# State-space blocks of 8 channels x 16 states, and experts with two input banks and one output bank, in a two-layer sandwich kernel

## The reference

```python
u, z = split(x @ W_in.T)
uc = silu(conv3(u) + conv_b)
proj = uc @ W_xproj.T            # B: 16 columns, C: 16 columns, dt: 8 columns
delta = softplus(dt @ W_dt.T + b_dt)
A = -exp(A_log)                  # 256 x 16
def step(h, inp):                # over the 1024 positions
    h = exp(d_t[:, :, None] * A) * h + (d_t * u_t)[:, :, None] * b_t[:, None, :]
    return h, einsum('bdn,bn->bd', h, c_t)
y = (ys + uc * D) * silu(z)
return y @ W_out.T
```

## Time and profile before

| | |
|---|---|
| runs, median of 3 (lowest, highest) | 3173.7 us (3173.47, 3174.76) |
| profiled execution, its own time | 3170.2 us |
| its span, first to last instruction | 3168.4 us |
| mean granted TensorE clock | 0.866 of full |
| PE busy | 2407.0 us (76%) |
| DVE busy | 2311.8 us (73%) |
| ACT busy | 1678.5 us (53%) |
| POOL busy | 1263.5 us (40%) |
| chain that ended last | PE 46%, DVE 20%, issue 18%, POOL 11%, ACT 4% |

### The profile page before, as it was taken

How to read it: one execution, slowest core, us unless ns; L and a number is a source line. 1 busy time by engine, 2 the same in 40 slices (tenths; PEclk the granted TensorE clock), 3 DMA queues, 4 the chain that set the end, 5 groups by cost and what they waited for, 6 DMA issues and landing times.

```text
span 3168.4 us, 41094 instructions
## 1 busy us (share of the span) xinstructions
PE 2407.0 (76%) x14962; PEld 1690.2 (53%) x14962; DVE 2311.8 (73%) x4141; ACT 1678.5 (53%) x2552; POOL 1263.5 (40%) x1203
## 2 busy tenths in 40 slices
PE   3114776667676696899999999999999388667867
PEld 1002444344344564577777777776777366245635
DVE  3994798699599612688878878887888533874386
ACT  4223663665376242678777877787778124022402
POOL 0341143144124200365766576667667540114011
PEclk8556878888788898799999999999999789788978
DMA  3000000000000000100000100010000100000000
GB/s 99 0 0 0 0 1 1 1 1 1 1 1 1 1 1 14 41 21 21 24 21 21 28 21 21 24 29 21 21 21 1 40 1 1 0 14 1 1 0 14
DMA packets 32026, 41.96 MB, mean 13 GB/s; under 512 B 8897, under 2 KB 18130, under 8 KB 31442
## 3 DMA queue, kind: packets, MB, share of 16 engines
q1 hardware_dynamic: 31826, 39.34, 4.6%
HBM read 12.05 MB, written 2.10 MB: 4 GB/s over the span
## 4 chain that ended last, share of the span: by engine, by line
PE 46%; DVE 20%; issue 18%; POOL 11%; ACT 4%; SPq 1%; DMA 1%; POOLq 0%; DVEq 0%; ACTq 0%
PE ps L954 10%; PE ps L932 6%; PE ps L943 6%; POOL MA L379 5%; PE ps L710 3%; DVE MA L1090 3%; DVE MA L1410 3%; PE ps L914 2%; DVE lnb L265 2%; PE ps L1724 2%; PE ps L645 2%; PE ps L1711 2%; PE ps L647 1%; PE ps L646 1%; PE ps L1648 1%
## 5 line engine op out<-in xcount | busy, mean ns | idle before, releaser
L1090 DVE TENSOR_REDUCE MA<-ps 128x1 f32<-128x1024 f32 x512 | 623.1, 1220 | 190.4 <-PE ps L932 177.6
L379 POOL TENSOR_TENSOR MA<-MA,BIG 128x1024 f32<-128x1024 f32 x120 | 280.1, 2355 | 624.3 <-DVE BIG L350 624.3
L954 PE MATMUL ps<-MA,WB 128*64 128x128 f32 x4096 | 504.5, 277 | 0.0
L954 PEld LDWEIGHTS ps<-MA,WB 128*64 128x64 f32 x4096 | 442.8, 137 | 88.4 <-issue 87.4
L344 DVE TENSOR_TENSOR_SCAN BIG<-BIG 128x1024 f32<-128x1024 f32 x128 | 346.8, 2748 | 0.0
L932 PE MATMUL ps<-BIG 96*128 96x512 f16 x1024 | 312.6, 387 | 13.3 <-DMA BIG<-WB 4.9
L632 ACT ACTIVATE HR<-ps,b 128x512 f32<-128x512 f32 x288 | 191.5, 686 | 244.0 <-PE ps L647 243.0
L710 PEld LDWEIGHTS ps<-WB,HR 128*128 128x128 f32 x2304 | 305.8, 209 | 25.0 <-issue 8.7
L710 PE MATMUL ps<-WB,HR 128*128 128x128 f32 x2304 | 312.8, 294 | 0.0
L1017 ACT ACTIVATE WB<-ps,MA 128x1024 f32<-128x1024 f32 x206 | 229.5, 1114 | 149.3 <-DVE MA L1090 147.5
L497 PE MATMUL ps<-bc,sel 96*128 96x512 bf16 x256 | 108.2, 520 | 249.1 <-DVE BIG L350 190.7
(11 more groups left out here) (286 smaller groups left out, 5133.2 us busy)
## 6 DMA issues: line engine op xcount, KB each, us to landing
BIG<-BIG SPq DMA_DIRECT2D x192, 64.0 KB, 2.0
BIG<-WB SPq DMA_DIRECT2D x192, 64.0 KB, 2.0
WB<-w_dram SPq DMA_DIRECT2D x1, 2304.0 KB, 14.6
X<-x_dram SPq DMA_DIRECT2D x4, 512.0 KB, 12.5
HR<-w_dram SPq DMA_DIRECT2D x1, 2048.0 KB, 9.3
out_dram<-X SPq DMA_DIRECT2D x4, 512.0 KB, 3.2
WB<-wqkv_dram SPq DMA_DIRECT2D x1, 1536.0 KB, 6.1
WB<-w_dram SPq DMA_DIRECT2D x2, 512.0 KB, 8.2
```

The source lines that it names most:

```text
L379: e.tensor_tensor(yy[:, c, :], yy[:, c, :], db[n % 2][c], ALU.add).then_inc(*p_my.up(b, n, c))
L954: x = e.matmul(bank[6][64 * pp:64 * pp + 64, 0:128], V[(4 * b + g) % 2][:, k, 64 * pp:64 * pp + 64], DT[n % 2][:, 128 * k:128 * k + 128], ...
L1090: e.tensor_reduce(L_of(n)[:, c:c + 1], ps[s][:, :], AX, ALU.max, negate=True).then_inc(*v_amx.up(n, s))
```

## The change

**Blocks instead of states.** The 256 x 16 pairs of a channel and a state are cut in 32 blocks `j` of 128 partitions, 8 channels with 16 states each. B and C no longer change from block to block: their 128-partition copies `Brep` and `Crep` are made once a batch by matmuls with repeated columns of `wx` (`bc`). What changes is delta and delta times u: both are split in three bf16 parts by ACT and POOL (`part`, `rest`), stored to DRAM, read back stacked as 96 partitions (`sin`), and broadcast to the 16 partitions of each channel by a matmul with `esel` (`dl` to bank 2, `du` to banks 0 and 1). ACT's exponential reads bank 2, half by half, and writes a ring of seven tiles. DVE multiplies by B in place in PSUM (`tb`), the scan reads its second operand from PSUM, POOL multiplies by C (`th`), and PE sums over the states with the f32 matrix `ysel` into banks 4 and 5 (`y`, for two blocks at a time). z and the convolved u are kept in DRAM between use and come back before the D term.

**One list of events.** `mamba_events` writes the planned times of all engines. The next batch's preparation is planned inside the loop of the batch before (30 us after its start), and the splitting of the expert weights inside the first loop. All small state-space matmuls share bank 2, each waiting for the reader before (`m_freed`). A loop is planned at 4.4 us a block in the first batch and 6.1 in the others; experts of batch b are planned from 36 us after its last block.

**Expert banks.** Inputs use banks 3 and 6 in turn, outputs bank 7 alone, so that the products of an expert wait for the sum of the one before.

The core of the diff:

```diff
-M_PERIOD, N_PERIOD = 181, 6.8
+S_AT, TT = [58.0], [4.4, 6.1, 6.1, 6.1]
+for _t in TT:
+    S_AT.append(S_AT[-1] + 32 * _t + 4)
+PRE_AT = [(0.0, 1.0), (S_AT[0] + 30, 2.0), (S_AT[1] + 30, 3.0), (S_AT[2] + 30, 3.0)]
-    return M_AT["rnorm"] + 1 + F_PERIOD * b + F_AT[what] + more
+    return S_AT[b] + 31 * TT[b] + 36 + F_AT[what] + more
...
+                for j in range(32):
+                    t = T0 + P * j
+                    for h in range(2):
+                        g = T0 + P * (j - j % 4) - 8.8 + 1.1 * (2 * (j % 4) + h)
+                        if b == 0 and j < 4:
+                            g = T0 - 1 + 0.1 * (2 * j + h)
+                        through(g, "dl", "a", b, j, h)
+                    at(t - 0.5, "pe", "du", b, j)
+                    at(t + 0.2, "dve", "tb", b, j)
+                    at(t + 1.4, "dve", "scan", b, j)
+                    at(t + 3.8, "pool", "th", b, j)
+                    if j % 2:
+                        at(t + 7, "pe", "y", b, j // 2)
...
+                    e.tensor_tensor(ps[0][:, :], ps[0][:, :], Brep, ALU.mult).then_inc(*v_mtb.up(b, j))
...
+                    e.tensor_tensor_scan(m_ring(b, j), m_ring(b, j), ps[0][:, :], 0.0, ALU.mult, ALU.add).then_inc(
+                        *v_mscan.up(b, j))
...
+                    e.tensor_tensor(m_ring(b, j), m_ring(b, j), Crep, ALU.mult).then_inc(*p_mth.up(b, j))
...
+                    e.activation(half_of(m_ring(b, j), h), PB, ACT.Exp, bias=0.0, scale=aneg[:, n:n + 1]).then_inc(*a_ma.up(b, j, h))
...
+                yield t
+                if m_freed.get(w):
+                    e.wait_ge(*m_freed[w])
...
+                    e.matmul(PB, esel[:, q, :], half_of(stk[:, j // 8 % 2, 0, j % 2, :], h), start=True, stop=True).then_inc(
+                        *t_mdl.up(b, j, h))
...
+                    o = earlier(b, j, 1)
+                    if o:
+                        e.wait_ge(*v_mscan.at(*o))
+                    for h in range(2):
+                        i = e.matmul(bank[h], esel[:, q, :], half_of(stk[:, j // 8 % 2, 1, j % 2, :], h), start=True, stop=True)
+                    i.then_inc(*t_mdu.up(b, j))
...
+                    e.wait_ge(*p_mth.at(b, 2 * m + 1))
+                    for h in range(2):
+                        for j in (2 * m, 2 * m + 1):
+                            c, n, q = block_of(j)
+                            i = e.matmul(Y2[32 * n:32 * n + 32, 512 * h:512 * h + 512], ysel[:, q, :], half_of(m_ring(b, j), h),
+                                         start=q == 0, stop=q == 3)
+                    i.then_inc(*t_my.up(b, m))
...
+        UP, DN = [bank[3], bank[6]], bank[7]
...
-                            elif PLAN[kk - 2][1] == 8:
-                                e.wait_ge(*a_facc.at(b, PLAN[kk - 2][0]))
+                            elif PLAN[kk - 1][1] == 8:
+                                e.wait_ge(*a_facc.at(b, PLAN[kk - 1][0]))
                             else:
-                                e.wait_ge(*v_fcb.at(b, kk - 2))
-                        o = bank[6 + kk % 2][:, 128 * j:128 * j + 128]
+                                e.wait_ge(*v_fcb.at(b, kk - 1))
+                        o = DN[:, 128 * j:128 * j + 128]
```

More of the change, by code:

```diff
@@ new lines, in program, with block_of @@
+        stk = MA[0:96, 8196:12292].bitcast(BF16).rearrange("p (s a i t) -> p s a i t", s=2, a=2, i=2)
+        dtb = lnb[0][0:8, :, :].rearrange("p j c -> p (j c)")
+        lnf = lnb[0][:, :, :].rearrange("p j c -> p (j c)")
+        R_ = big[0:7]
+        Brep, Crep = big[7], big[8]
+        yy = [SEL[:, 2048 * c:2048 * c + 2048].bitcast(F32) for c in range(2)]
+        zt = BC[:, 0:2048].bitcast(F32)
+        wx = small["wx"]
+        PB, Y2 = bank[2], ps[2]
+        def block_of(j):
+            return j // 16, 2 * (j // 8 % 2) + j % 2, j // 2 % 4
@@ new lines, in program, with mamba_bank @@
+        p_mrs, p_mrest = [tick(f"p_mrs{i}", NB) for i in range(2)], tick("p_mrest", NB, 2, 2, 2)
+        p_mth, p_mx = tick("p_mth", NB, 32), tick("p_mx", NB)
+        s_zu, s_back, s_stk = [[sem(f"{x}{i}") for i in range(2)] for x in ("s_zu", "s_back", "s_stk")]
+        s_part = [sem(f"s_part{i}") for i in range(4)]
+        def mamba_bank():
+            freed, last = {}, None
+            for _, eng, w in M_EVENTS:
+                if eng != "pe" or w[0] in ("du", "y"):
+                    continue
+                freed[w] = last
+                last = {"xt": a_mxt, "in": a_mev, "dt": a_mdt, "wd": a_mve, "bc": a_mbc, "dl": a_ma, "out": a_mout}[w[0]].at(*w[1:])
+            return freed
@@ L208, in const_pool, with part_of, m_ring, earlier @@
+        m_freed = mamba_bank()
+        def part_of(b, c, s, a):
+            n = 6 * (2 * b + c) + 2 * s + a
+            return n % 4, n // 4
+        def m_ring(b, j):
+            return R_[(32 * b + j) % 7]
+        def earlier(b, j, n):
+            j = 32 * b + j - n
+            return (j // 32, j % 32) if j >= 0 else None
         def const_pool(e):
@@ L1792, in _ @@
             load(e)
+            mamba_sp(e)
             attention_sp(e)
@@ L1832, in layout @@
     r["ident"] = np.eye(128, dtype=np.float32)
+    place = np.eye(32, dtype=np.float32)
+    r["esel"] = np.tile(np.repeat(place, 16, axis=1), (3, 1))
+    r["ysel"] = np.repeat(place.reshape(4, 8, 32).transpose(1, 0, 2), 16, axis=0)
     r["iota8"] = np.broadcast_to(np.arange(8, dtype=np.float32), (128, 8))
```

784 lines of the change are left out of this document (462 added, 322 removed).

## The result

The changed kernel takes **3482.7 us** (median of 4 runs, 3481.9 to 3486.5) against 3173.6 us: a ratio of 1.098, 95% interval 1.096 to 1.0998, slower by 309 us. The forecast was 3097 us, range 3010 to 3180. The first layer now ends at 1560.6 us (last residual) instead of 1249; what lies behind it takes 1919 us as before, so the whole loss is in the first layer.

A forecast was written before the change was run, and what follows sets the result against it. DVE work was taken to bound the loops and latency the gaps; 84 + 175 + 735 + 9 + 19 + 150 = 1172 us against 1249, -77, gave 3097 us, range 3010 to 3180.

The forecast's parts named there:

- DVE, single durations: State blocks on DVE: scan 2.27 us, product with B in PSUM 1.21 us, 3.48 us a block.
- rival (3): DVE's product in PSUM costs 2.4 us, +38 us a batch; kernel 3167 us, about no change; chance 0.06.
- Start: Before the first loop: statistics 13 us earlier, offset by input matmuls (+5) and splitting (about +8); loop still at 84 us.
- First loop: First batch's state loop: 32 blocks of 4.2 us, plus preparation and sum stalls; 175 us (ends 150 and 215) against 166.6.
- Coupling: Batches two to four: ScalarE and TensorE overlap partly, between 625 and 807 us; taken 735, 245 a batch.
- Table loads: ScalarE, first layer: 216 loads against 129 now, 1.283 us each with no extra drain.
- Rival (1): Sums over states overlap in different 32-column strips, at half the cost; -157 us, kernel 3017 us; chance 0.26.
- Rival (2): ScalarE and TensorE take turns in full, TensorE slowed to 1.2 GHz for a time; +100 us, kernel 3274; chance 0.11.
- point of decision: Batches two to four: the slower rival decides from 271 us a batch (812 in three), where the sum is 1249.
- Experts' single output bank: Experts: waiting for the four adds of the expert before (1.1 us) fits in the 2.9 us of the next products.
- Tail: Behind the last scan: 9 us to the gate, 19 to the fourth batch's residual, 150 for the experts alone.
- Signs of being wrong: First layer: a batch over 271 us, the first batch's D term after 300, or a scan not shorter.

The follow-up runs named there:

- g4: Changed kernel with experts behind the last state loop, delta rows in pairs behind the rows of delta times u, two delta banks: 3442.2 us.
- e5: Changed kernel with experts behind the last state loop and delta rows evenly spread half by half instead of eight in a row: 3506.7 us.
- e8: Changed kernel, experts beside the loops as before, delta rows evenly spread half by half instead of eight in a row: 3393.2 us.
- e6: Changed kernel with experts behind the last state loop, groups of eight delta rows kept, delta rows in banks 3 and 6 in turn: 3479.3 us.
- e3: Changed kernel, order only: experts of all four batches planned behind the last state loop: 3606.7 us.
- e1: Changed kernel with the experts' gelu replaced by the identity: 3280.1 us.
- f3: Changed kernel, order only: four delta halves, for two blocks, behind every second row pair of delta times u: 3421.4 us.
- g3: Changed kernel with delta rows evenly spread and 36 of a batch's 64 matmuls for the sums over states left out: 3371.6 us.
- e4: Kernel before the change, with only the experts' outputs all put in bank 7: 3212.5 us.
- f4: Changed kernel, experts behind the last loop, delta rows evenly spread, eight unread matmuls added behind each row pair of delta times u: 3542.1 us.

## Why the prediction was wrong

By its steps, the sum of 1172 against 1560.6. The sum's marks are the last scans, and the table's the gates; by the sum's own marks the terms are 84, 175, 735, 9, 19 and 150 forecast, and 104, 220, 1053, 7, 25 and 152 measured:

- **DVE, single durations**: right. Scan 2.27 forecast, 2.285 measured, no long ones; product 1.21, 1.23; so rival (3) did not occur. The exponential from PSUM takes 0.687, not 0.60 (22 us of ACT in the layer).
- **Start**, 84 forecast, 104 measured. The term of the eight input matmuls through one bank, 13.7 us, was 22 us: a step is 2.76 us (2.07 of matmul, where I had 0.85, then 0.60 and handovers). 2.07 us is what such a pair lasts where the granted clock is 0.5, but the profile grants 1.00 in this stretch (30 to 52 us), so the reason stays open. The two traces place the rest: the statistics came 12 us earlier, as forecast, the first transposes took 2 us longer, and from the last input eviction to the first product with B it is 52 us in place of 35, 17 more where I had 8. (The term's own parts give 13.2 us, not 13.7.)
- **First loop**, 175 forecast from the first product to the last scan (ends 150 and 215), 220 measured (104.0 to 323.7; 248 to the gate). The chain of 4.7 us is right (g4: 4.75), but I priced it as if only that chain stood in the way. The delta rows of four blocks in one piece cost 20 us (e5, e8), their one bank some 30 to 40 (e6, g4), and in PE's order the rows of delta times u stand behind both.
- **Coupling**, the step that failed: "I take 735, a little over the middle"; 1031 measured from gate to gate (342, 380, 309), 1053 from last scan to last scan. Even its upper end, 807 for full turns, was too low. Two things were missing. The first is the loop itself: I priced a batch by the busy sums of ACT and PE and took the loop (175 us for the first one) to lie under them, but e3 shows 720 us for the three loops with no expert beside them, 240 a loop. The second is the price of the experts beside them, 311 us more; without gelu (e1) the same three stretches take 830, so only 110 more. In the third batch's six groups I had ACT's 99 us in the windows and PE's 127 in the gaps, 226. They are 126.8 and 143.7, 270.5: in a window the bank's handovers come on top of ACT's work (ACT 81% busy), and PE fills the gap to 92%. The rest of that batch is 110 us where I had 54, 77 of them between the gate and the first window with experts beside: there the last experts' sums, norms and gating stand among the scans (DVE busy 57 of 77), which my window count did not hold. (The parts that I gave for PE's work add up to 211 us, not 214; that moves nothing.)
- **Table loads**: their number was right and their duration too (1.283). The error was to count them as ACT's work only. Between one delta row and the next they are PE's and DVE's time too: 203 us back without gelu (e1), for 222 us of loads. Their count alone does not price them: 127 loads less between e8 and f3 gave nothing.
- **Rival (1)**: its mechanism is true, four sum matmuls take 1.91 us at full clock and 3.63 at half, a little over half of my 3.4 and 6.8. It moved little: the sums were not what the batches waited for (22 us in g3).
- **Rival (2)**, chance 0.11, named the part of the mechanism that lies beside the experts: loads stand between PE and its next bank, ACT and PE take turns, PE's clock falls in the windows (0.58 to 0.82 on average, between its levels of 1.2 and 2.4 GHz), and the kernel is slower. What the lower clock cost there no run separates. It gave 3274; the other 209 us are the windows and gaps above, the start and the first loop. Its point of decision, 271 us a batch, rested on a start of 84 and a loop of 175; with the measured start, first loop and tail it is 240. The 344 us measured on average are over either.
- **Experts' single output bank**: "those fit in the 2.9 us", true in the changed kernel (3.3 us of wait), not in the kernel before (39 us, e4), where DVE is full.
- **Tail**: 9 forecast from the last scan to the gate, 19 from there to the residual and 150 for the experts; 7, 25 and 152 measured.
- **Signs of being wrong**: two of my three came, batches over 271 us and a D term of the first batch after 300 (346.7); the third, a scan no shorter than before, did not.

## What to carry to other kernels

When one bank carries data between two engines, count the longest thing that the order puts between a fill and the next fill, on both engines, and then everything behind it in the queue of the engine that fills: a 1.28 us load there costs three engines, and beside full work it costs little (17 us for 111 loads in the kernel before). Busy sums of 60 to 80% on every engine are no sign of room if the work comes in alternating pieces. Ask first what each stream takes with the other absent (one run with the two apart tells it: 249 and 256 us here, against a forecast of 245 for both together). Then compute piece by piece, window plus gap, including the pieces in which the second stream is absent. And price a pooled resource where it is used: the same output bank costs 39 us beside a full DVE, and beside an idle one it makes PE wait 3 us.

## What the runs showed of the hardware

- A load follows an activation and is followed by the next at once: gelu ends 957.01, load 957.02, exponential 958.32. The Trainium skill ("ScalarE: Activation LUTs", What ACT_TABLE_LOAD costs) asks 1.38 us more for a drain; as in the earlier trace rows, the trace shows none; the 90 loads before exponentials are 1283 ns each.
- Matmuls with 32 output columns that go to two column strips in turn run at about twice the rate of others: eight 32-bit instructions in 1.91 us (3.63 at half clock), where two of 128 columns take 1.02. By the Trainium skill ("TensorEngine Tiling (Array Packing)", Key Properties) different tiles can execute in parallel, and this agrees. The narrow form is not cheap by itself: in g3 a sum matmul of 32 columns often stands alone, and its two instructions take 1.04 us, as much as 128 columns. In the changed kernel the eight instructions start in pairs, 0.01 us apart within a pair and about 0.43 between pairs. The first row is the changed kernel's, the second g3's:

```profile
444.77 1.91 PE L677 MATMUL ps<-BIG,ysel 128*32 128x512 f32 x8
...
801.47 1.04 PE L677 MATMUL ps<-BIG,ysel 128*32 128x512 f32 x2
```

- POOL's product takes 2.34 us alone and up to 3.33 while DVE works on SBUF tensors. DVE's convolution step takes 1.28 alone, and beside POOL's product either POOL is the longer one (3.30, with DVE's step at 1.26: 870.2 us) or DVE is (3.26, with POOL's product at 2.84: 854.8 us). The scan, with one operand in PSUM, stays at 2.29 or less. The contention of the earlier trace rows has moved from the scan to the preparation.
- The granted clock in the first loop is 0.65, with PE busy 155 of 248 us in short pieces: more time at 1.2 than at 2.4 GHz; filler matmuls brought it to 0.87 (f4).
